# Attention over 128 pairs: how the key norms are summed, and who adds the weighted values

## The reference, cut to what matters

```python
q, k, v = (cproj(Wq), cproj(Wk), cproj(Wv))        # complex, 16 heads of 64
qr = q * phase[None];  kr = k * phase[None]
E = jnp.exp(jnp.clip(-mu[:, None, None] * dt[None], MIN_EXP, 0.0))
s = jnp.einsum('bihd,bjhd->bhij', qr, jnp.conj(kr)).real
qn = (q.real ** 2 + q.imag ** 2).sum(-1).transpose(0, 2, 1)
kn = (k.real ** 2 + k.imag ** 2).sum(-1).transpose(0, 2, 1)     # key norms
maha = jnp.maximum(qn[..., None] + (E * E)[None] * kn[:, :, None, :] - 2.0 * E[None] * s, 0.0) / V[None]
logits = coef * jnp.log1p(maha / nu[None, :, None, None]) - 0.5 * DH_ * jnp.log(V)[None]
A = jax.nn.softmax(jnp.where(causal[None, None], logits, -jnp.inf), axis=-1)
out = jnp.einsum('bhij,bjhd->bihd', A.astype(v.dtype), v)
y = jnp.concatenate([out.real..., out.imag...], axis=-1)
x = x + y @ Wo                                     # the weighted values are added to x
```

## Time and profile before

| | |
|---|---|
| median of 3 runs | 1696.05 us (1693.87 to 1697.52) |
| span of the profiled execution | 1693.8 us, clock of PE granted at 0.998 of full on average |
| PE busy | 1642.7 us (97%), 9690 matmuls |
| DVE busy | 1483.9 us (88%) |
| ACT busy | 1452.4 us (86%) |
| POOL busy | 974.3 us (58%) |
| `square` on ACT (L1406), 127 of them | first at 259.0, last at 1451.9 us |

### The profile page before, as it was taken

One profiled execution on the slowest core, in us unless ns is written; L12 is line 12 of the kernel. 1 busy time (PEld: TensorE's weight loads), 2 busy tenths in 40 slices (PEclk: granted clock), 3 DMA queues, 4 the chain that ended last, 5 costly groups with the idle time before them and its releaser, 6 DMA issues. The chain is left out here.

```text
span 1693.8 us, 30993 instructions
## 1 busy us (share of the span) xinstructions
PE 1642.7 (97%) x9690; PEld 1337.0 (79%) x9690; DVE 1483.9 (88%) x3380; ACT 1452.4 (86%) x2909; POOL 974.3 (58%) x826
## 2 busy tenths in 40 slices
PE   5999988999999999999999999999999999899998
PEld 4787866888888888888788888888887887777876
DVE  6878877999899989999999998999899989977665
ACT  6677678999999999999999999999999999765765
POOL 3564546566566656665655565566566656345565
PEclk9999999999999999999999999999999999999999
DMA  6000032232223322232232323232332222100000
GB/s 177 1 1 1 1 103 66 63 91 62 77 70 75 74 68 79 63 78 65 77 79 63 91 57 82 54 91 60 82 79 63 69 70 51 26 7 7 13 11 15
DMA packets 50482, 100.03 MB, mean 59 GB/s; under 512 B 8208, under 2 KB 25872, under 8 KB 50320
## 3 DMA queue, kind: packets, MB, share of 16 engines
q1 hardware_dynamic: 50320, 98.07, 22.5%
HBM read 17.95 MB, written 5.24 MB: 14 GB/s over the span
## 5 line engine op out<-in xcount | busy, mean ns | idle before, releaser
L1495 POOL TENSOR_TENSOR early<-early 128x1024 f32<-128x1024 f32 x127 | 303.2, 2387 | 470.0 <-PE pS L1183 258.6
L654 POOL TENSOR_TENSOR hid_lo_d<-hid_d,hid_hi_d 128x512 fp32r<-128x512 f32 x176 | 231.5, 1316 | 218.7 <-ACT hid_hi_d L559 212.1
L1387 ACT ACTIVATE early<-early,qnorm 128x128 f32<-128x128 f32 (+3 forms) x512 | 247.0, 554 | 68.3 <-DVE early L1578 66.4
L1183 PE MATMUL pS<-early 128*128 128x128 f32 (+3 forms) x1024 | 297.6, 433 | 0.3 <-PEq L105 0.3
L1371 ACT ACTIVATE early<-early,nmax 128x128 f32<-128x128 f32 (+3 forms) x512 | 281.6, 562 | 6.9 <-DVE nmax L1565 6.7
L1183 PEld LDWEIGHTS pS<-early 128*128 128x128 f32 x1024 | 164.7, 191 | 96.0 <-issue 61.4
L1574 DVE SCALAR_TENSOR_TENSOR pS<-pS,ek 128x1280 f32<-128x1280 f32 x128 | 191.4, 1495 | 55.3 <-PE pS L1183 54.4
L1504 POOL TENSOR_TENSOR ek<-early 128x128 f32<-128x128 f32 (+3 forms) x256 | 216.7, 881 | 3.6 <-ACT early L1379 3.0
L1504 POOL TENSOR_TENSOR ek<-decay,early 128x128 f32<-128x128 f32 (+3 forms) x256 | 215.3, 876 | 0.0
L1400 ACT ACTIVATE early<-early,params 128x512 f32<-128x512 f32 (+1 forms) x256 | 196.9, 819 | 0.0
L1198 PEld LDWEIGHTS pV<-ones,early 128*128 128x128 f32 x1016 | 134.3, 193 | 61.3 <-issue 61.3
(11 more groups left out here) (394 smaller groups left out, 3883.7 us busy)
## 6 DMA issues: line engine op xcount, KB each, us to landing
early<-early SPq DMA_DIRECT2D x263, 256.0 KB, 3.6
early<-trig_d SPq DMA_DIRECT2D x64, 64.0 KB, 2.0
trig_d<-early SPq DMA_DIRECT2D x3, 1024.0 KB, 6.9
early<-in_w SPq DMA_DIRECT2D x3, 704.0 KB, 9.0
x_sb<-in_x SPq DMA_DIRECT2D x4, 512.0 KB, 8.4
early<-in_wqk SPq DMA_DIRECT2D x16, 128.0 KB, 3.4
cos<-trig_d SPq DMA_DIRECT2D x32, 64.0 KB, 2.3
sin<-trig_d SPq DMA_DIRECT2D x32, 64.0 KB, 2.1
```

The source lines that it names most:

```text
L654: g.tensor_tensor(hid_lo[:, par], hid[:, par], hid_hi[:, par].bitcast(F32), ALU.subtract).then_inc(lo_done, 1)
L1183: last = pe.matmul(s.pS[:, span(I)], rot[:, I * P:(I + 1) * P], rot[:, N:N + (I + 1) * P], start=True, stop=True)
L1387: last = a.activation(u[:, span(I)], u[:, span(I)], ACT.Relu, bias=qnorm[:, r % 2, I:I + 1])
L1495: g.tensor_tensor(rot[:], by_cos[:], crossed[:], ALU.add).then_inc(S["rot_done"], 1)
```

## The change

Two parts of a pair's work move between the engines.

**Key norms.** The squares of the keys are split in two fp32r parts. DVE casts the high part (`high_squares`), POOL subtracts it from the square (`low_squares`), and PE adds up both parts by ones in two fp32r matmuls in place of the one in full fp32. In `norms` the query squares now come first and the key parts behind them, after a wait for `key_lo`. `high_squares(n+1)` stands between the two halves of `peaks(n-1)` and waits for `square(n+1)`. `low_squares(n+1)` is the first thing that POOL does in a step. `square` now waits for `kn_done`.

**Weighted values.** For the pairs of the first 15 heads, one DVE product of 512 columns (`scale_share`, into the tile `share`) stands ahead of `distances`, and POOL adds `share` to x (`add_share`), between `low_squares` and `rotate`. `weigh` then waits for `scaled_done`. The last head keeps `accumulate`.

**Room.** The two parts of the squares lie in the low half of the second feed-forward weights, `w2s[1]`. Its first 1024 columns go to DRAM before the attention stage and come back at its end.

```diff
@@ sync, first feed-forward stage
                 sp.wait_ge(w2_lo, len(PIECES2))
+                sp.dma_start(s.w2_lo_d, s.w2s[1][:, 0:2 * N].bitcast(F32)).then_inc(s.S["w2_lo_out"], 16)
                 sp.dma_start(wv_raw, s.wv.rearrange("h d k -> d h k")).then_inc(wvo_in, 16)
@@ tensor, down(e)
+                if last_phase and e == 0:
+                    pe.wait_ge(s.S["w2_lo_in"], 16)
@@ sync, attention
+                if i * 16 + r == PAIRS - 1:
+                    sp.wait_ge(S["kn_done"], PAIRS)
+                    sp.dma_start(s.w2s[1][:, 0:2 * N].bitcast(F32), s.w2_lo_d).then_inc(S["w2_lo_in"], 16)
@@ tensor, norms(i, r)
-                pe.matmul(s.p6[:], s.ones[:], squares[:, N:2 * N], start=True, stop=True).then_inc(S["kn_done"], 1)
                 for I in range(TILES):
                     last = pe.matmul(s.p5[:, I:I + 1], squares[:, I * P:(I + 1) * P], s.ones[:, 0:1],
                                      start=True, stop=True)
                 last.then_inc(S["q2_done"], 1)
+                wait(pe, S["key_lo"], n)
+                pe.matmul(s.p6[:], s.ones[:].bitcast(F32R), key_hi, start=True, stop=False)
+                pe.matmul(s.p6[:], s.ones[:].bitcast(F32R), key_lo, start=False, stop=True).then_inc(S["kn_done"], 1)
@@ tensor, weigh(i, r)
-                wait(pe, S["acc_done"], n)
+                wait(pe, S["scaled_done"], min(n, LAST_HEAD))
+                if n > LAST_HEAD:
+                    pe.wait_ge(S["acc_done"], n)
@@ scalar, square(i, r)
-                wait(a, S["q2_done"], n)
+                wait(a, S["kn_done"], n)
@@ gpsimd
+            def add_share(i, r):
+                n, b = i * 16 + r, r % B
+                x_b = s.x_sb[:, b * TILES:(b + 1) * TILES, :]
+                g.wait_ge(S["scaled_done"], n + 1)
+                g.tensor_tensor(x_b, share[:], x_b, ALU.add).then_inc(S["acc_done"], 1)
+
+            def low_squares(i, r):
+                n = i * 16 + r
+                g.wait_ge(S["key_hi"], n)
+                g.tensor_tensor(key_lo, squares[:, N:2 * N], key_hi.bitcast(F32), ALU.subtract).then_inc(S["key_lo"], 1)
+
             def a_step(i, r):
                 if live(i, r + 1):
+                    if (i, r) != (0, -1):
+                        low_squares(i, r + 1)
+                    if live(i, r - 3) and i * 16 + r - 3 < LAST_HEAD:
+                        add_share(i, r - 3)
                     if (i, r) != (0, -1):
                         rotate(i, r + 1)
@@ vector, peaks(i, r), called with r - 1
                 for k, (_, pieces) in enumerate(HALVES):
+                    if k == 1 and live(i, r + 2):
+                        high_squares(i, r + 2)
                     v.wait_ge(S["ln_done"], 2 * n + k + 1)
@@ vector
+            def high_squares(i, r):
+                n = i * 16 + r
+                if n == 1:
+                    v.wait_ge(S["w2_lo_out"], 16)
+                v.wait_ge(S["sq_done"], n + 1)
+                v.tensor_copy(key_hi, squares[:, N:2 * N]).then_inc(S["key_hi"], 1)
+            def scale_share(i, r):
+                n = i * 16 + r
+                v.wait_ge(S["av_done"], n + 1)
+                v.wait_ge(S["rinv_done"], n + 1)
+                wait(v, S["acc_done"], n)
+                v.tensor_tensor(share[:], s.p7.rearrange("p (i d) -> p i d", i=TILES),
+                                rinv[:, r % 4, :].unsqueeze(2).broadcast_to([P, TILES, P]),
+                                ALU.mult).then_inc(S["scaled_done"], 1)
@@ vector, a_step
                     if live(i, r - 3):
-                        accumulate(i, r - 3, range(TILES // 2))
+                        if n - 3 < LAST_HEAD:
+                            scale_share(i, r - 3)
+                        else:
+                            accumulate(i, r - 3, range(TILES // 2))
                     distances(i, r)
...
-                if live(i, r - 3) and n != PAIRS:
+                if live(i, r - 3) and n != PAIRS and n - 3 >= LAST_HEAD:
                     accumulate(i, r - 3, range(TILES // 2 if live(i, r) else 0, TILES))
```

More of the change, by code:

```diff
@@ L1051, in attention_phase @@
         squares, rot, knorm, u, z = s.squares, s.rot, s.knorm, s.u, s.z
+        key_hi, key_lo = s.key_sq
         qnorm = sb("qnorm", [P, 2, TILES])
@@ L1060, in attention_phase @@
         rinv = sb("rinv", [P, 4, TILES])
+        share = sb("share", [P, TILES, P])
         stats = sb("stats_at", [P, TILES, 6])
@@ L1087, in attention_phase @@
         HALVES = ((slice(0, N), ORDER[:2]), (slice(N, SW), ORDER[2:]))
+        LAST_HEAD = (H - 1) * B
         LATE = slice(6 * TILES, 8 * TILES)
@@ L1593, in accumulate @@
                 v.wait_ge(S["rinv_done"], n + 1)
+                if n == LAST_HEAD:
+                    v.wait_ge(S["acc_done"], n)
                 for I in tiles:
@@ L1725, in a_step @@
                     peaks(i, r - 1)
+                if i == 0 and r == 0:
+                    high_squares(i, r + 1)
                 if i == 0 and r in (1, 2):
@@ L1782, in program @@
         s.trig_d = nc.dram_tensor("trig_d", [3, H, DH // 2, N], F32, kind="Internal").ap()
+        s.w2_lo_d = nc.dram_tensor("w2_lo_d", [P, 2 * N], F32, kind="Internal").ap()
         s.x_sb = sb("x_sb", [P, TT, D])
@@ L1787, in program @@
         s.w2s = [sb(f"w2_{h}", [P, HC * P], F32R) for h in ("hi", "lo")]
+        s.key_sq = tuple(s.w2s[1][:, k * N:(k + 1) * N] for k in range(2))
         s.wr = sb("wr", [P, 2 * NE], F32R)
@@ L1819, in program @@
                  "val_done tr_done trc_done av_done rinv_done acc_done stat_done dve_passed pool_passed sp_passed "
-                 "late_stat late_mv late_var late_ln late_root late_rstd late_step late_xn late_xt late_hi late_lo mv_done expanded0 expanded1")
+                 "late_stat late_mv late_var late_ln late_root late_rstd late_step late_xn late_xt late_hi late_lo mv_done expanded0 expanded1 "
+                 "w2_lo_out w2_lo_in key_lo key_hi scaled_done")
         s.S = {n: ctx.enter_context(nc.semaphore(n)) for n in names.split()}
```

## The result

| | before | after |
|---|---|---|
| median, runs taken side by side | 1696.78 us (1693.87 to 1698.77, 4 runs) | 1898.13 us (1897.50 to 1898.76, 4 runs) |
| span of the profiled execution, clock | 1693.8 us, 0.998 | 1896.1 us, 0.995 |
| steps between two `square`, odd head | 8.70 | 10.76 |
| the same, plain step of an even head | 10.04 | 10.76 |
| 16 steps | 150.31 | 176.50 |

What follows compares the result with a forecast made beforehand. A ring of ACT and DVE through the cast's wait for `square`, lengthened by POOL, was to bound every step at 10.89 us; 16 steps with tables 180.7 against 150.3, 239 us more over 126 steps: 1935 us, range 1770 to 1985.

Steps and rivals of the forecast that it cites:

- The ring: ACT's `clamp` to `square`, then DVE's cast, `peaks`, product and `distances` back to `clamp`: 9.82 us, 10.89 with POOL's hold-up.
- The turns: POOL's `low_squares` and DVE's second half of `peaks`, both operands in SBUF, alternate by whole instructions: 1.07 us more every step.
- Rival 1: `low_squares` and `peaks` don't hold each other up; the step is 9.82 us, the time 1777 us; chance 13%.
- Rival 2: POOL's `spread` beside `peaks` passes the cast and delays most steps: 11.4 to 11.8 us, about 2025 us; chance 9%.
- Rivals 3 and 4: PE's clock falls behind its waits, well over 2300 us, 3%; or ACT runs ahead and work decides, 1665 us, 5%.
- work decides: Engines' busy time alone sets the step: 9.65 us in even steps, some 8.6 in odd ones.
- Head tables: Building two heads' tables in 16 steps adds 2.5 us on ACT and 4 us on DVE, range 2 to 7.
- The narrower range: The forecast's own range for the median time, with 10.7 to 11.2 us for the ring: 1900 to 1975 us.
- A sign that was wrong: DVE was to stand idle ahead of the cast, released by `square`, and PE to wait 1.5 us before the key matmuls.
- PE's gain: Two fp32r key-norm matmuls replace one fp32: 0.39 us less PE time a step, 25 us over 64 even steps.

Runs made afterwards that it cites:

- e4: The whole change, but POOL's `low_squares` subtracts only 4 of its 512 columns, the rest of the low part left out: 1774.19 us, ratio 1.046 to the kernel before.
- e5: The whole change, but `low_squares` on POOL also waits until both halves of `peaks` are through: 1845.14 us, ratio 1.087 to the kernel before.
- e10: The whole change, but the last product of `spread` on POOL is 4 columns wide instead of 256: 1888.54 us, ratio 1.112 to the kernel before.
- e3: The whole change, but DVE's cast stands behind both halves of `peaks` instead of between them: 1823.05 us, ratio 1.075 to the kernel before.
- e6: Only the key norms split, the cast behind both halves of `peaks`, weighted values as before: 1725.76 us, ratio 1.018 to the kernel before.
- e11: Against the kernel before, key norms split only in seven even-head steps of each 16, cast behind `peaks`, weighted values as before: 1687.43 us, ratio 0.995.

## Why the prediction was right

Direction, place and mechanism held in plain steps, as they were put. What the head tables cost was mis-sized, and one of the signs named was wrong.

- **The ring.** Both kinds of step were to become equal, and are: 10.76, where 10.89 was summed. Of the 0.13 too much, 0.06 is the signal from `square` to the cast (0.03 instead of 0.09), and 0.08 the turn: 0.99 in the ring instead of 1.07. `clamp` to `square`, cast, product and `distances` came within 0.02 of their terms.
- **The turns.** `peaks` of 256 columns take 1.48 (1.5 was said), `low_squares` 1.70 (1.6 was said). That POOL and a DVE instruction with two SBUF operands take turns, whole instructions at a time, stood on one row; e4 shows it by the width of POOL's instruction alone, and e5 by a wait that makes the kernel faster.
- **Rival 1** is what e4 runs: 1777 was said for a ring without turns, 1774 is measured. That this is so close is partly luck: the ring is 0.06 a step shorter than the 9.82 said, and the tables cost 4.4 in 16 steps (160.53 - 16 x 9.76) in place of 3.5. The change itself is 124 us above it, so it is out.
- **Rival 2** (POOL late, at 2025) is out in plain steps: DVE was through with the first half of `peaks` 0.04 us ahead of the cast (791.94 and 0.54, its length to the next start in the earlier trace rows, against 792.52), where 0.1 was said, and e10 shows that nothing was paid for it there. In steps with tables POOL did reach into the ring, 10 us in all.
- **Rivals 3 and 4**: the clock was 0.995, and nothing became faster. That it didn't fall was not safe: in e3 and e5, with PE waiting longer for the low part, it did in 29 and 19 steps. That work decides (9.65 and 8.6 us a step) was wrong for every order tried: the shortest odd step with the split that a fall of the clock didn't precede took 9.12 (e6).
- **Head tables**, the term that was mis-sized: 6.5 us in 16 steps said, 176.50 - 16 x 10.76 = 4.3 measured. With the ring (16 x 0.13 = 2.1) that makes up the 4.2 us between 180.7 and 176.5; 4.2 / 16 x 126 = 33 us, most of the 37 by which 1935 was too high. The narrower range, 1900 to 1975, left out that these terms can be low or high together: with its own bounds of 10.7 and 11.2 for the ring and 2 and 7 for the tables on DVE the sum runs from 1896 to 1998.
- **A sign that was wrong.** DVE was to be idle ahead of the cast. It wasn't, though the prediction's own figures (10.8 and 10.89) had left it only 0.1. Who looks for the wait in the list of waits finds 10.6 us and would take `square` for harmless. PE waited 0.81 ahead of the key matmuls instead of 1.5, since `scores` and the query norms were themselves late; the rest of its slack lay ahead of the transposes (1.0) and in them (1.49 to the next start in an odd step, 1.12 before).
- **PE's gain.** The split frees 0.40 us of PE (0.39 said): 0.86, 0.81 and 0.32 from the key norms to the second matmul of `project` against 0.81, 0.32, 0.23 and 0.23 in e11; of that 0.10 to 0.19 in a step reached the time in the best case, and none in the change.

## What to carry over

Ahead of moving a piece to an idle engine, close the rings: from one instruction through all that wait for each other back to the same instruction of the next step; the longest ring is the step, whatever the shares of busy time say. A piece with two SBUF operands on POOL isn't in parallel with such an instruction on DVE, nor with a DVE cast from SBUF to SBUF, so add the two up as one resource, and start POOL's piece where DVE reads PSUM. When two paths end together the list of waits hides one of them; shorten the other to see it.

## What the runs showed of the hardware

- The first fp32r matmul behind the single-column query norms takes 0.32 us to the next start, the ones behind it 0.23. The split took that dearer first place over from `project`, so the pair costs 0.55 and frees 0.40.
- In e3 PE stood 1.73 us for the low part at one place, and the granted clock had fallen to half, 1.2 GHz, when it went on at 747.92; the step took 11.46 us instead of 10.15, and the next one 9.14. Behind another wait of 1.75 us (at 737.79) it didn't fall. In the change itself, with waits of 0.8 and 1.0, it stayed at full. What makes it fall behind one wait and not behind the other is open. Windows of e3 (length, PE busy, PEclk, DMA):

```profile
747.00:747.60 0.60, 0.00 (x0) 0.89 0.00 0
747.60:748.00 0.40, 0.08 (x1) 0.50 0.00 0
748.00:749.00 1.00, 1.00 (x3) 0.50 0.00 0
...
750.00:751.00 1.00, 1.00 (x4) 0.56 0.00 0
751.00:752.00 1.00, 1.00 (x10) 1.00 0.00 0
```

- A VectorE instruction that is held ends about its reading time after POOL does: 0.29 us for 256 columns (794.73 to 795.02), 0.41 for 384. The Trainium skill, page "SBUF — State Buffer", section "Who interferes with whom", has the rule of whole instructions, and e4 and e5 agree (1.48 against 0.48).
- The same section states that a cast in a two-port mode contends with GpSimd as well, and the trace agrees that a cast is held (in which mode it ran no row shows). In the steps that build a head's tables, a DVE cast of 256 columns with one operand, in SBUF, falls beside `spread` and takes 1.09 to 1.11 us, all 15 times; in the kernel before it runs when POOL is through and takes 0.26 or 0.27. The product of 512 columns on POOL in the rows below starts at 657.17 and is over at about 658.5 (the 256 columns behind it take 0.75, as at 769.60), and the cast ends at 658.61. A DVE `tensor_scalar` of 512 columns does the same (1.24 against 0.46, at 646.22 and 591.32). So what POOL holds up is wider than the prediction's "both operands in SBUF". The cast of `high_squares` took 0.41 to 0.46 in every run; in the plain steps POOL stood idle then. In the change, in the kernel before:

```profile
657.17 2.03 POOL L1517 TENSOR_TENSOR ek<-early 128x512 f32<-128x512 f32 x2
```

```profile
657.51 1.10 DVE L1559 CAST wqk_hi<-early 128x256 fp32r<-128x256 f32 x1
```

```profile
601.36 0.26 DVE L1531 CAST wqk_hi<-early 128x256 fp32r<-128x256 f32 x1
```
